# A fused attention and FFN kernel: when its weights are loaded, and who issues the first copies

## What is computed

```python
x = L0_attn_hidden                                   # (4, 2048, 256) f32
x = x + attn(layernorm(x), Wq, Wk, Wv, Wo)           # 16 heads of 16, causal window of 64
x = x + ffn(layernorm(x), W1, b1, W2, b2)

# attn: scores = q k^T / 4 + bias (allowed: j <= i and j > i - 64), softmax, times v, times Wo^T
# ffn:  Wq1, Wq2 = ternary(W1), ternary(W2); relu(x Wq1^T + b1) Wq2^T + b2
def _quantize(W):
    gamma = jnp.mean(jnp.abs(W))
    return jnp.clip(jnp.round(W / (gamma + EPS)), -1.0, 1.0)
```

## Time and profile before

| | |
|---|---|
| median of 3 runs | 692.32 us (688.95 to 693.97) |
| profiled execution | 693.37 us, span of its trace 691.6 us |
| PE busy | 645.2 us, 93% |
| DVE busy | 627.6 us, 91% |
| ACT busy | 625.5 us, 90% |
| POOL busy | 618.7 us, 89% |
| mean granted clock of PE | 0.99 of full speed |

### The profile page before, as it was taken

One profiled execution on the slowest core, in us unless ns is written; L12 is line 12 of the kernel. 1 busy time (PEld: TensorE's weight loads), 2 busy tenths in 40 slices (PEclk: granted clock), 3 DMA queues, 4 the chain that ended last, 5 costly groups with the idle time before them and its releaser, 6 DMA issues.

```text
span 691.6 us, 24467 instructions
## 1 busy us (share of the span) xinstructions
PE 645.2 (93%) x8038; PEld 550.8 (80%) x8038; DVE 627.6 (91%) x1596; ACT 625.5 (90%) x2649; POOL 618.7 (89%) x869
## 2 busy tenths in 40 slices
PE   6578779999999999999999999999999999998887
PEld 4356568888888889888888888888878888887776
DVE  4689889999999999999999999999999999898854
ACT  5689899999999999999999999999999999898833
POOL 8288999999999999999999999999999999999920
PEclk9989999999999999999999999999999999999999
DMA  8767556465756656474756657474755646363000
GB/s 286 106 84 104 74 93 75 76 84 74 123 73 102 96 98 97 77 94 71 124 73 101 96 97 102 71 99 68 128 71 97 73 91 76 52 87 67 18 31 31
DMA packets 497988, 61.17 MB, mean 88 GB/s; under 512 B 470724, under 2 KB 493510, under 8 KB 497864
## 3 DMA queue, kind: packets, MB, share of 16 engines
q1 hardware_dynamic: 486744, 50.53, 51.1%
q10 hardware_dynamic: 11120, 9.09, 4.6%
HBM read 11.86 MB, written 8.39 MB: 29 GB/s over the span
## 4 chain that ended last, share of the span: by engine, by line
PE 43%; POOL 31%; issue 10%; ACT 8%; DVE 6%; SPq 1%; DMA 1%; POOLq 0%; ACTq 0%; DVEq 0%
POOL p L391 13%; PE ps L1097 10%; POOL tl L415 9%; PE ps L1085 7%; PE ps L991 6%; PE ps L971 5%; POOL th L409 5%; ACT p L494 4%; PE ps L1030 4%; PE ps L1058 3%; PE ps L1043 3%; PE ps L1070 1%; SPq L278 1%; POOL rstdA L375 1%; ACT hTh L571 1%
## 5 line engine op out<-in xcount | busy, mean ns | idle before, releaser
L494 ACT ACTIVATE p<-ps,negm 128x96 f32<-128x96 f32 x1024 | 341.9, 379 | 6.1 <-DVE negm L713 5.4
L494 ACT ACTIVATION_READ_ACCUMULATOR p<-ps,negm 128x1 f32 x1024 | 251.7, 247 | 0.0
L415 POOL TENSOR_TENSOR tl<-pt,th 128x384 f16<-128x384 f32 x256 | 235.1, 918 | 16.4 <-ACT th L503 2.1
L391 POOL TENSOR_TENSOR p<-p,rden 128x384 f32<-128x384 f32 x256 | 214.3, 837 | 8.6 <-DVE rden L720 8.2
L726 DVE STREAM_TRANSPOSE pt<-p 128x384 f32<-128x384 f32 x256 | 141.6, 553 | 14.1 <-POOL p L391 12.4
L713 DVE TENSOR_REDUCE negm<-ps 128x4 f32<-128x384 f32 x256 | 136.1, 532 | 8.8 <-PE ps L971 6.0
L971 PE MATMUL ps<-k,qbd 128*128 128x96 f16 x1536 | 124.1, 207 | 3.2 <-ACT p L494 3.2
L971 PEld LDWEIGHTS ps<-k,qbd 128*128 128x128 f16 x1536 | 105.0, 98 | 13.0 <-ACT p L494 3.6
L571 ACT ACTIVATE hTh<-ps 128x512 f16<-128x512 f32 x128 | 79.9, 625 | 20.8 <-PE ps L1085 19.5
L991 PE MATMUL ps<-th,vb 128*128 128x96 f16 (+1 forms) x1120 | 97.9, 203 | 0.7 <-issue 0.5
L1085 PE MATMUL ps<-xTCh,w1T 128*128 128x256 f16 x512 | 97.6, 272 | 0.8 <-ACT xTCh L566 0.8
(11 more groups left out here) (139 smaller groups left out, 1479.3 us busy)
## 6 DMA issues: line engine op xcount, KB each, us to landing
k<-kst SPq DMA_DIRECT2D x32, 288.0 KB, 4.1
vb<-vd SPq DMA_DIRECT2D x256, 32.0 KB, 2.6
out<-x SPq DMA_DIRECT2D x32, 256.0 KB, 2.7
qbd<-qs SPq DMA_DIRECT2D x254, 32.0 KB, 2.3
x<-in_L_attn_hidden ACTq DMA_DIRECT2D x15, 512.0 KB, 5.8
kw<-kst SPq DMA_DIRECT2D x31, 192.0 KB, 3.9
k<-kst SPq DMA_DIRECT2D x31, 144.0 KB, 3.4
vb<-in_L_ffn_W SPq DMA_DIRECT2D x2, 1024.0 KB, 8.8
```

What stands on the lines that cost most here:

```text
L391: e.tensor_tensor(p3, p3, rden[n % 4][:, :].unsqueeze(2).to_broadcast([128, 4, 96]), ALU.mult).then_inc(s_nm, 1)
L415: e.tensor_tensor(tl[g % 2][:, o], pt[n % 3][:, :], th[g % 2][:, o], ALU.subtract).then_inc(s_lo, 1)
L494: ins = e.activation(p[:, 96 * u:96 * u + 96], bank[:, 96 * u:96 * u + 96], ACT.Exp, bias=m[:, u:u + 1], accum_out=r[:, u:u + 1])
```

## The change

Nothing is computed otherwise. W1 and W2 are issued by SP behind the first queries and keys, not ahead of them. Wo is issued by ACT in slot 1, transposed on PE in slot 4, split in slot 5. x2 is issued in slot 2; its statistics move to slots 5 and 6, those of x1 to slots -9 and -8. Of the 12 first copies of q (half t = 0), SP issues 8 and ACT 4; it was 10 and 2. The fold constants and the low half of the biases move ahead of the scores. Wq's transposes go to banks 0 and 1. The magnitudes move one slot back, and with them the sums, the mean and the thresholds.

```diff
-N_STATS, N_RSTD, N_NORM = ((-7, 0, 10), (-6, 1, 16)), (-5, 5, 23), ((0, 9, 23), (0, 11, 24))
+N_STATS, N_RSTD, N_NORM = ((-9, 5, 10), (-8, 6, 16)), (-7, 7, 23), ((0, 9, 23), (0, 11, 24))
+W_BANK = (0, 1, 6, 7, 6, 7, 6, 7)
-W_ABS, W_TERNARY, W_FOLD = (1, 2, 3, 4), (6, 8, 10, 12, 14, 16, 18, 20), (15, 16, 17, 18, 19, 20)
+W_ABS, W_TERNARY, W_FOLD = (2, 3, 4, 5), (6, 8, 10, 12, 14, 16, 18, 20), (15, 16, 17, 18, 19, 20)
...
 # SP
-            e.dma_start(n1, w1_d.rearrange("(t p) d -> p t d", p=128)).then_inc(d_w["1"], 16)
-            e.dma_start(n2, w2_d.rearrange("(t p) f -> p t f", p=128)).then_inc(d_w["2"], 16)
             for n in SLOTS:
...
-                        place_q(e, c, t, ((0, 1, 2, 3), (0, 1, 2, 3), (0, 1, 2, 3) if c or t else (2, 3)))
+                        place_q(e, c, t, ((0, 1, 2, 3), (0, 1, 2, 3), (0, 1, 2, 3) if c or t else ()))
...
+                if n == A_K[0] + 2 - 16:
+                    e.dma_start(n1, w1_d.rearrange("(t p) d -> p t d", p=128)).then_inc(d_w["1"], 16)
+                    e.dma_start(n2, w2_d.rearrange("(t p) f -> p t f", p=128)).then_inc(d_w["2"], 16)
...
 # ACT
                 if n == -16:
                     load_x(1)
                     weights(range(4))
-                    e.dma_start(nat["o"], wo_d.rearrange("(t p) d -> p t d", p=128)).then_inc(d_w["o"], 16)
-                    e.wait_ge(s_wlo, 4)
-                    load_x(2)
                 if n == -12:
                     weights(range(4, 6))
                     masks()
-                if n == -6:
+                if n == 1:
+                    e.dma_start(nat["o"], wo_d.rearrange("(t p) d -> p t d", p=128)).then_inc(d_w["o"], 16)
+                if n == 2:
+                    e.wait_ge(s_wlo, 4)
+                    load_x(2)
+                if n == 5:
                     weights(range(6, 8))
 
                 if n == A_K[0] + 2 - 16:
-                    place_q(e, 0, 0, ((), (), (0, 1)))
+                    place_q(e, 0, 0, ((), (), (0, 1, 2, 3)))
...
 # DVE
-                if n == -6:
+                if n == 5:
                     weights(range(6, 8))
-                if n == 2:
+                if n == -8:
                     fold_consts()
+                if n == -7:
                     bias_low()
-                if n == W_TERNARY[0] - 2:
+                if n == W_TERNARY[0]:
                     sums()
-                if n == W_TERNARY[0]:
+                if n == W_TERNARY[0] + 1:
                     thresholds()
...
 # PE
-                if held is None and bank < 4:
+                if held is None and bank < 6:
                     return banks[bank]
-                if held is None and bank < 6:
-                    e.wait_ge(s_wlo, 2)
-                elif held is None:
+                if held is None:
...
-                if n == -9:
+                if n == 4:
                     weights(range(6, 8))
-                if n == W_TERNARY[0]:
+                if n == W_TERNARY[0] + 1:
                     mean()
```

More of the change, by code:

```diff
@@ L471, in weights @@
                     e.wait_ge(s_wp, w + 1)
-                    e.activation(wT[n][0][:, t, :], banks[4 + w if w < 4 else 6 + w % 2][:, 0:256], ACT.Copy,
+                    e.activation(wT[n][0][:, t, :], banks[W_BANK[w]][:, 0:256], ACT.Copy,
                                  scale=WS * (0.25 if n == "q" else 1.0)).then_inc(s_whi, 1)
@@ L671, in weights @@
                 for w in ws:
-                    n, t, bank = "qkvo"[w // 2], w % 2, banks[4 + w if w < 4 else 6 + w % 2]
+                    n, t, bank = "qkvo"[w // 2], w % 2, banks[W_BANK[w]]
                     hi, lo, src = wT[n][0][:, t, :], wT[n][1][:, t, :], bank[:, 0:256]
@@ L913, in ternary @@
                 if j == 0:
+                    e.wait_ge(s_wlo, 8)
                     e.wait_ge(d_w["1"], 16)
```

## The result

| | before | after |
|---|---|---|
| median of 10 runs each | 692.86 us (688.95 to 696.21) | 697.62 us (695.80 to 699.74) |
| profiled execution | 693.37 us, span 691.6 us | 699.06 us, span 697.2 us |
| PE, DVE, ACT, POOL busy | 645.2, 627.6, 625.5, 618.7 us | 651.2, 630.9, 625.7, 619.7 us |
| mean granted clock of PE | 0.990 | 0.973 |

The changed kernel is slower: ratio 1.0065, 95% interval 1.0045 to 1.0085, that is 4.8 us by the medians. The prediction had a gain of 2.7 us.

The account below looks back on a forecast made before the run. It took the chain of waits over the start as the bound: slot 7 ending on DVE at 43.3 instead of 46.05 gains 2.7 us, so the median 692.32 becomes 689.6 us; range 686.6 to 693.2.

Parts of the forecast that it names:

- The step that failed: After slot 7: same order on all engines, V's copies leave SP earlier by as much, so the 2.7 us gain stays.
- I cost these at nothing: DVE's chunk 1 statistics, fold constants and bias, hidden by waits and POOL's clearing: 0 us, at worst the bias' 1.48.
- W1's landing: W1's load, issued by SP at 20.35, lands 5.3 us later at 25.7; other end 7.4 us, at 27.8.
- ACT's sum: ACT from the first magnitude's start to the fifth exponential group's end: 10.9 us, ending at 36.6 against 39.29.
- The mean's wait: DVE before slot 7's end: threshold matmul done on PE at 38.4, no wait; 0.9 us at PE's lower clock.
- no wait of PE for Wo: Sign expected in the new trace: PE never waits for Wo, wanted at about 33 and landed before.
- First scores: Start of chunk 0's scores on PE: at 21.6 (20.6 to 24), four and a half us earlier.
- Banks: Wq in banks 0 and 1 removes PE's 0.80 us wait; SP's first issue goes from 14.25 to 13.45.
- (c): Rival: ACT's doubled issuing stalls SP's first copies, W1 lands at 30.7; 2.3 us slower, 694.6; chance 0.10.
- (a): Rival: W1 lands late, at 27.8, with PE at the lower clock; no gain, 692.6; chance 0.15.
- (b): Rival: W1 is there when ACT asks (24.2), landing within 3.9 us; gain 4.2, 688.1; chance 0.15.
- The rule beside the rows: DMA engines alternate between queues, so Wo takes half the turns; W1 lands 0.7 us later, gain 2.0, median 690.3.

Follow-up runs that it names:

- e1: Changed kernel with W1 and W2 issued at the head of SP's queue again, ahead of the first queries; 692.95 us, ratio 0.9999.
- e6: Kernel before with only the banks of the weights' transposes changed (Wq in banks 0 and 1); 695.28 us, ratio 1.0006.
- e8: Changed kernel with W1 and W2 at the head of SP's queue and the mean's matmul ahead of q and k on PE; 691.83 us, ratio 0.9970.
- e3: Changed kernel with the mean's matmul moved ahead of q and k of chunk 1 on PE; 697.82 us, ratio 1.0064.
- e2: Changed kernel with W1 and W2 issued by ACT behind its k and kw copies instead of by SP; 697.37 us, ratio 1.0059.
- e11: Changed kernel with W1 at SP's head, W2 still late, mean's matmul ahead of q and k, fold constants and bias in slots 3 and 4; 695.70 us, ratio 1.0028.
- e9: As e8, with the fold constants in slot 3 and the low half of the biases in slot 4; 691.33 us, ratio 0.9951.
- e12: As e9, with 1 MB more (x4 and x5, loaded an extra time) on SP's queue behind the first keys; 695.17 us, ratio 1.0020.
- e4: Changed kernel with the fold constants and the low half of the biases back in slot 2; 695.97 us, ratio 1.0052.
- e5: Changed kernel with Wo issued by ACT in slot -16 again, its transposes staying in slot 4; 698.48 us, ratio 1.0069.

## Why the prediction was wrong, step by step

**The step that failed** is the one with no number of its own: "Beyond slot 7 the order is the same on all engines; the copies of V leave SP earlier by as much." I followed SP's queue up to the loads that the change had moved, and not the eight copies, two keys and 16 copies of V behind them. The earlier trace rows had shown the effect, 5.75 us for four copies while large loads run. I used it to price the copies that get rid of the loads, and not those that get them. I had also read it wrong: those four copies were not issued at 300 to 400 GB/s, which the earlier trace rows has up to 17.25 us, but at 71 to 199 in nearly all of their stretch, and W1 and W2 had landed by then (5.93 + 7.4 = 13.3, 6.37 + 10.2 = 16.6); Wo and x2 on ACT's queue were still moving. In eleven of the fourteen kernels of the table the first product with V starts 1.89 to 1.95 us after V's last issue; in the other three (e1, e6, e8) it starts 2.4 to 4.2 us after it, something else being last there. The kernel before is among the eleven (1.93): V's hour was the edge before the change too, with 0.52 us of idle PE as its only trace and nothing lost by it at slot 12. The errors at slot 7 below add up to more (5.2 us, from a lead of 2.7 to a lag of 2.4), but they do not make the time: e3 wins 2.1 us there and nothing at slot 12. Putting the loads back (e1) takes the whole of the 4.8 us away, doing so on another queue (e2) nothing, and leaving W2 alone there (e11 against e9) or moving another MB there (e12 against e9) brings a like loss: that the place of the loads sets V's hour, and V's hour the loss, is shown; what holds an issue back is not.

**"I cost these at nothing"** (fold constants and bias) was wrong, and so was its bound of 1.48 us. The cover was POOL's clearing, and DVE's operation does not run beside that: 3.48 us instead of 0.22. POOL's rstd took 2.31 us beside DVE's bias instead of 1.01. Together they made the normalisation of chunk 1 3.5 us later than in e4. The sizes are shown by e4, with e1 for the clearing, and so is that they did not matter for the time in the changed kernel, where W1 and V come later. With the loads at the head the clearing plays no part (0.21 us in e1 and e8); what is left of it, the bias beside rstd and DVE's work ahead of the first scores, is worth 1.4 us at slot 7 from e8 to e9, and the ratios 0.9970 and 0.9951 have intervals that overlap.

**W1's landing**, "I take 5.3", was 7.9 us, past even the other end of 7.4. ACT's sum was right: 10.9 us predicted from the first magnitude to the end of the fifth group, 39.55 - 28.84 = 10.7 measured. So the lead that ACT was to have at 36.6 was lost by the mis-sized landing (2.6 us) and 0.55 of a later issue.

**The mean's wait**, "0, other end 0.9", was 1.70 us; e3 takes it away, 2.1 us at slot 7. PE at 0.50 was the other end's reason and explains the smaller part. The matmul, "done at 38.4", started at 43.62, because PE came to slot 6's scores near 39 and not at 33.6: it had stood 1.76 us for DVE's low half of Wo, until 38.02, ahead of the first ternary transposes. Besides, 33.6 and the 3.57 us of the earlier trace rows give 37.2; the prediction names no source for the other 1.2 us. And the sign "no wait of PE for Wo" failed: 4.92 us, from Wo's 9.7 us to landing counted from 23.77. e5 takes that wait away, and slot 7 stays (46.85).

**First scores**: 22.65 against "21.6". The copies and their issue were right (5.53 us for eight, first at 13.07). ACT's kw, taken as the last to land, was issued at 17.55 and needed 4.5 us and not 3.4; for the 0.6 us between 22.05 and the first scores the trace names the copies into qm, and I leave them open.

**Banks**: SP's first issue at 13.07 against 13.45, but e6 shows that the banks alone don't bring it; which other part of the change they need was not tried.

**The rivals.** (c) had the sign, with an issue stall on SP, but for the first copies and because of ACT's issues beside them. Those did not stall. (a) had the late W1 right, and nothing beyond it. (b) was far off with 7.9 us of landing; "less than any large load of the trace" was not so either, one load of x, 0.5 MB, landed in 3.7. None had the copies behind the loads. The rule beside the rows, turns between queues, was applied to Wo against W1 and not to the small copies. The range does not follow from its terms: 688.1 and 692.6 with 1.3 us on either side are 686.8 and 693.9, not 686.6 and 693.2; 697.62 lies outside both.

## What to carry to other kernels

A large load that is moved to a later place does not leave the busy stretch, it takes it along: price it by the small transfers that are issued while it moves, on any queue, down to the first use of the last of them. An edge in a trace may have half a microsecond of idle time or none as its sign; before counting a gain to the end, ask for each stream behind the change when its last piece is wanted. And work put "beside" another engine is free only if a row shows the two side by side.

## What was unexpected in the hardware

- Issuing a 32 KB copy on SP takes 0.66 to 0.70 us when nothing holds it. With 2 MB of loads issued just ahead eight of them took 11.9 to 13.5 us in six kernels, with 1 MB 9.2 to 10.8 in three, with none 5.7 to 7.5 in five. The engine that issues the 2 MB makes no difference (12.71, 12.80).
- 3.48 us for a 128x128 conversion on DVE beside POOL's clearing, until that ended; 0.22 alone. (The Trainium skill, SBUF — State Buffer, SBUF: two separate sides, has DVE and GpSimd share a pair of ports as a lock held for a whole instruction, the other one blocked. The trace agrees that DVE stands blocked, 15.57 + 3.48 = 19.05 against the clearing's end at 18.98, but not for one instruction: the clearing is four of 0.95 us back to back, from 15.35 on, and DVE came through only behind the last.) It works the other way too: POOL's 128x4 operation took 2.31 us beside DVE's bias and 1.01 without it.
- W1, 1 MB, issued when no other large load was moving, but with W2 right behind it and Wo and x2 3 to 4 us later, took 7.9 us to land (7.8 from ACT's queue in e2), more than the 7.4 us among all the loads of the start.
